# Routed experts' biases: from a one-hot matmul to broadcast rows added by VectorE, and a turning moved behind the next block's rows

## What is computed

```python
y = gelu(einsum('bsd,edf->bsef', x, g) + gb)      # rgb: [16, 256]
y = y * (einsum('bsd,edf->bsef', x, w1) + b1)     # rb1: [16, 256]
out = einsum('bsef,efd->bsed', y, w2) + b2        # rb2: [16, 512]
```

## Time and profile before

| | us |
|---|---|
| time before, median of 3 (1360.68 to 1362.64) | 1361.8 |
| the profiled execution | 1362.64 |
| its span in the trace | 1360.8 |
| TensorE busy in the span | 1321.8 (97%) |
| VectorE busy | 850.3 (62%) |
| ScalarE busy | 687.1 (50%) |

### The profile page before, as it was taken

One profiled execution on the slowest core, in us unless ns is written; L12 is line 12 of the kernel. 1 busy time (PEld: TensorE's weight loads), 2 busy tenths in 40 slices (PEclk: granted clock), 3 DMA queues, 4 the chain that ended last, 5 costly groups with the idle time before them and its releaser, 6 DMA issues. The chain is left out here.

```text
span 1360.8 us, 22755 instructions
## 1 busy us (share of the span) xinstructions
PE 1321.8 (97%) x6836; PEld 1102.7 (81%) x6836; DVE 850.3 (62%) x1753; ACT 687.1 (50%) x1615; POOL 384.3 (28%) x353
## 2 busy tenths in 40 slices
PE   6899999999999999999999999997999999999997
PEld 3667777888888888888888888886887888888886
DVE  5788755666666666666666777666666444344568
ACT  3334427666666666666666776663312323232232
POOL 0336465000013092030550302800032232323164
PEclk9999999999999999999999999999999999999999
DMA  9999989967677769696687899793646999894375
GB/s 290 382 343 375 369 299 319 341 223 237 205 276 272 237 231 327 206 341 207 226 301 268 289 316 329 278 354 146 246 156 244 336 347 363 289 368 172 128 235 171
DMA packets 160057, 375.57 MB, mean 276 GB/s; under 512 B 23164, under 2 KB 80576, under 8 KB 147696
## 3 DMA queue, kind: packets, MB, share of 16 engines
q1 hardware_dynamic: 144416, 314.32, 66.0%
q0 software_dynamic: 15568, 60.32, 12.5%
HBM read 245.84 MB, written 128.22 MB: 275 GB/s over the span
## 5 line engine op out<-in xcount | busy, mean ns | idle before, releaser
L1193 ACT ACTIVATE a_pr<-a_pr,a_stat 128x128 f32<-128x128 f32 (+3 forms) x256 | 141.9, 555 | 71.4 <-DVE a_stat L1272 71.4
L1212 ACT ACTIVATE a_pT<-x_banks 128x512 fp32r<-128x512 f32 (+1 forms) x192 | 87.1, 531 | 75.6 <-PE x_banks L1415 75.6
L1199 ACT ACTIVATE a_pr<-a_pr,a_stat 128x128 f32<-128x128 f32 (+3 forms) x256 | 122.3, 550 | 0.5 <-DVE a_stat L1277 0.5
L1399 PE MATMUL x_banks<-a_pT,a_cv 128*128 128x512 f32 (+1 forms) x576 | 120.5, 354 | 0.3 <-issue 0.3
L1399 PEld LDWEIGHTS x_banks<-a_pT,a_cv 128*128 128x128 f32 x576 | 103.4, 188 | 21.2 <-issue 0.7
L1272 DVE CUSTOM_DVE_ANT_0 a_pr<-a_psS,f_mask 128x256 f32<-128x256 f32 (+2 forms) x192 | 101.2, 555 | 23.7 <-PE a_psS L1387 23.3
L1300 DVE TENSOR_TENSOR a_pT<-x_banks,a_pT 128x512 fp32r<-128x512 f32 (+1 forms) x192 | 103.4, 594 | 12.6 <-ACT a_pT L1212 12.6
L101 PE MATMUL x_banks<-a_hT,a_wqk 128*128 (+1 forms) x256 | 99.9, 390 | 1.0 <-DVEq L1259 1.0
L102 PE MATMUL x_banks<-a_hT,a_wqk 128*128 (+1 forms) x256 | 99.7, 390 | 0.0
L103 PE MATMUL x_banks<-a_hT,a_wqk 128*128 (+1 forms) x256 | 99.6, 389 | 0.0
L1288 DVE SCALAR_TENSOR_TENSOR a_qT<-x_banks,a_qT 128x512 fp32r<-128x512 f32 x64 | 44.3, 692 | 85.6 <-ACT a_qT L1203 85.6
(11 more groups left out here) (378 smaller groups left out, 3611.9 us busy)
## 6 DMA issues: line engine op xcount, KB each, us to landing
w1s_d<-a_ws SPq DMA_DIRECT2D x72, 512.0 KB, 3.5
a_wqk<-wqk_d SPq DMA_DIRECT2D x64, 512.0 KB, 5.0
a_mh<-mhl_d SPq DMA_DIRECT2D x32, 1024.0 KB, 5.9
s_ring<-w1s_d SPq DMA_DIRECT2D x16, 2048.0 KB, 10.0
w2s_d<-a_ws SPq DMA_DIRECT2D x72, 256.0 KB, 3.9
qpe_d<-p_qs SPq DMA_DIRECT2D x16, 1024.0 KB, 5.1
a_rw<-in_L_ffn_rw SPq DMA_DIRECT2D x128, 128.0 KB, 3.5
a_qpe<-qpe_d SPq DMA_DIRECT2D x64, 256.0 KB, 2.7
```

The costliest lines, as they stand in the source:

```text
L1193: nc.scalar.activation(pr[i], pr[i], ACT.Exp, bias=nmax[:, i:i + 1], scale=-1.0, accum_out=rsum[:, i:i + 1]).then_inc(ex, 1)
L1199: nc.scalar.activation(pr[i], pr[i], ACT.Copy, scale=rinv[:, i:i + 1]).then_inc(nr, 1)
L1212: nc.scalar.activation(pT[:, u, 0, dst], src, ACT.Copy).then_inc(p_hi, 1)
L1399: last = nc.tensor.matmul(two_of(bank)[:, :, (2 - k) * P:2 * P], cv[:, j, cs], pT[:, :, ps, o:o + k * P], start=m == 0, stop=m == len(part ...
```

## The change

- **Biases.** `oh`, `bs`, the matmuls of lines 2419 and 2430, the making of `bs` ahead of the blocks and the one-hot row on ScalarE are gone. Instead SyncE loads, for each expert, 128 equal rows of its two first biases (tile `bg`, 128x512, 256 KB, from a new HBM tensor `b1_d` that holds both side by side) and of its second bias (`bo`, 128x512, 256 KB), into rings of three places as for the weights. The weights count as landed only with their biases.
- **VectorE** reads the place of the expert into a register (`row_of`, twice in a block), adds the bias to the gate part (into `y2`), adds it to the up part (into `y3`), multiplies `y3` with the gelu's result, and adds the second bias as it copies the result rows. The gelu reads and writes `y2` in SBUF.
- **Turning.** The two transposes of a block's activations (`turned`) move from the end of step k to step k+1, behind the four transposes of the rows of block k+2 and ahead of its first matmuls.
- The tiles `ys` and `lt` now lie in `bo`; the last updates of the shared experts use another temporary, with waits of their own; the second biases of the first three experts are loaded after the shared experts' last activations.

The diff, cut to its core:

```diff
+                def bias2(one, s, landed):
+                    sp.dma_start(bo[:, s], K.ins["L0_ffn_rb2"][one].broadcast_to([P, D])).then_inc(landed, 16)
+                def bias1(one, s, landed):
+                    sp.dma_start(bg[:, s], K.b1_d[one].broadcast_to([P, 2 * F])).then_inc(landed, 16)
...
                     sp.dma_start(ring1[:, s].rearrange("p c s n -> p (c s n)").bitcast(F32),
                                  K.w1s_d[bass.ds(e, 1)].rearrange("a p c s n -> (a p) (c s n)")).then_inc(rw1_in[s], 16)
+                    sp.wait_ge(gu_ok, done)
+                    bias1(bass.ds(e, 1), s, rw1_in[s])
...
+                    sp.wait_ge(yo_ok, done)
+                    bias2(bass.ds(e, 1), s, rw2_in[s])
...
-                    nc.scalar.activation(y2[:, u % 2], pg[:, u % 2, 0, 0:F], ACT.Gelu).then_inc(eg, 1)
+                    act.wait_ge(g_ok, k + 1)
+                    nc.scalar.activation(y2[:, u % 2], y2[:, u % 2], ACT.Gelu).then_inc(eg, 1)
...
+                def row_of(table, k):
+                    n = dve.value_load(slot[0:1, bass.ds(k, 1)], min_val=0, max_val=RS - 1)
+                    return table[:, bass.ds(n, 1)].rearrange("p a n -> p (a n)")
                 def rows(k, j, u):
+                    bias = row_of(bo, k)
                     dve.wait_ge(oo, k + 1)
...
-                    v.tensor_copy(yo[:, u % 2], po[:, u % 2]).then_inc(yo_ok, 1)
+                    tt_(yo[:, u % 2], po[:, u % 2], bias, ALU.add).then_inc(yo_ok, 1)
...
+                    bias = row_of(bg, k)
+                    dve.wait_ge(fo, k + 1)
+                    tt_(y2[:, u % 2], pg[:, u % 2, 0, 0:F], bias[:, 0:F], ALU.add).then_inc(g_ok, 1)
...
+                    tt_(y3[:, u % 2], pg[:, u % 2, 0, F:2 * F], bias[:, F:2 * F], ALU.add).then_inc(gu_ok, 1)
+                    dve.wait_ge(gu_ok, k + 1)
                     dve.wait_ge(eg, k + 1)
-                    tt_(y2[:, u % 2], pg[:, u % 2, 0, F:2 * F], y2[:, u % 2], ALU.mult).then_inc(em, 1)
+                    tt_(y2[:, u % 2], y3[:, u % 2], y2[:, u % 2], ALU.mult).then_inc(em, 1)
...
-                    pe.wait_ge(oh_ok, k + 1)
-                    nc.tensor.matmul(pg[:, u % 2, 0], oh[:, u], bs[:, 0], start=False, stop=True).then_inc(fo, 1)
...
-                    nc.tensor.matmul(po[:, u % 2], oh[:, u], bs[:, 1], start=False, stop=True).then_inc(oo, 1)
...
                     if k + 1 < NBLK:
                         trans(k + 1, (k + 1) // XS, (k + 1) % XS)
+                    if k:
+                        turned(k - 1, (k - 1) % XS)
                     ahead = gated(k, u, e, s)
```

More of the change, by code:

```diff
@@ L1556, in stage_ffn @@
         yo = N.t[:, 0:2]
-        y2 = N.t[:, 3].rearrange("p (u f) -> p u f", u=2)
+        y2, y3 = (N.t[:, n].rearrange("p (u f) -> p u f", u=2) for n in (3, 2))
         rev = small[:, 0:E]
@@ L1688, in _ @@
                 sp.wait_ge(taken, 1)
+                sp.wait_ge(b1_out, 32)
+                for e in range(RS):
+                    bias1(slice(e, e + 1), e, pre1_in[e])
                 weights(None, ring2[:, 0], 0, None, pre2_in[0])
-                sp.wait_ge(pre1_in[0], 16)
+                sp.wait_ge(y_lo, 2 * NU)
+                for e in range(RS):
+                    bias2(slice(e, e + 1), e, pre2_in[e])
+                sp.wait_ge(pre1_in[0], PRE1)
                 sp.sem_inc(landed1, 1)
-                sp.wait_ge(pre2_in[0], 16)
+                sp.wait_ge(pre2_in[0], 32)
                 sp.sem_inc(landed2, 1)
@@ L2412, in gated @@
                         nc.tensor.matmul(pg[:, u % 2, 0], xT[:, u % 2, 0, c], w(c, 1), start=False, stop=False)
-                        nc.tensor.matmul(pg[:, u % 2, 0], xT[:, u % 2, 1, c], w(c, 0), start=False, stop=False)
+                        last = nc.tensor.matmul(pg[:, u % 2, 0], xT[:, u % 2, 1, c], w(c, 0), start=False, stop=c == DC - 1)
                         if c == 1 and k + 1 < NBLK:
@@ L2417, in gated @@
                             ahead = (ahead, place(k + 1))
[L2418 to L2419 removed]
+                    last.then_inc(fo, 1)
                     return ahead
@@ L2428, in out, with turned @@
                         nc.tensor.matmul(po[:, u % 2], eT[:, u % 2, 0, f], w(f, 1), start=False, stop=False)
-                        nc.tensor.matmul(po[:, u % 2], eT[:, u % 2, 1, f], w(f, 0), start=False, stop=False)
-                    nc.tensor.matmul(po[:, u % 2], oh[:, u], bs[:, 1], start=False, stop=True).then_inc(oo, 1)
+                        last = nc.tensor.matmul(po[:, u % 2], eT[:, u % 2, 1, f], w(f, 0), start=False, stop=f == FC - 1)
+                    last.then_inc(oo, 1)
+                def turned(k, u):
+                    pe.wait_ge(em, k + 1)
+                    for f in range(FC):
+                        m = nc.tensor.transpose(py[:, f * PB:(f + 1) * PB], y2[:, u % 2, f * P:(f + 1) * P], K.ident[:, :])
+                    m.then_inc(et, 1)
                 def step(k, e, s, old):
@@ L2444, in step @@
                         part(1, 3, (3,)).then_inc(sh_o, 1)
-                    pe.wait_ge(em, k + 1)
-                    for f in range(FC):
-                        m = nc.tensor.transpose(py[:, f * PB:(f + 1) * PB], y2[:, u % 2, f * P:(f + 1) * P], K.ident[:, :])
-                    m.then_inc(et, 1)
                     return ahead
```

65 lines of the change are left out of this document (26 added, 39 removed).

## The result

The changed kernel takes **1350.97 us** (median of 1350.35 to 1353.39) against 1362.22 of the kernel before beside it: ratio 0.9928, 95% interval 0.9912 to 0.9943. The medians lie 11.3 us apart; by the ratio it is 9.8 us less, with 7.8 and 12.0 as the ends. A second series on another chip gave 1351.7 against 1360.39, ratio 0.9936 (0.9922 to 0.9951). The forecast was 1348, the range 1341 to 1358: right in direction and range, and 3 us too fast.

A forecast was written before the change was run, and what follows sets the result against it. TensorE was taken to bound the kernel, through its chain of turnings in the routed experts. Terms: -21.4 + 1 + 3.5 + 0.5 + 2 + 0.5 = -13.9, from 1361.8 to 1348 us; range 1341 to 1358.

The forecast's parts named there:

- Matmuls removed: TensorE, routed experts: 47 blocks lose two matmuls each, 94 x 0.228 = 21.4 us less; block goes to 4.77 us.
- The longer way to the product: VectorE's added bias additions before the product: no stall in most blocks, 1 us more allowed, bounds 0 to 9 us.
- product always late: Rival: each block's turning waits 0.2 us for VectorE's product, 9.2 us instead of 1, so 1356 us; chance 0.12.
- the text's own sign: Wrong on the product if the turning of the activations waits for VectorE in ordinary blocks.
- The slack of 0.12 to 0.27 us: Margin between the product's end and TensorE asking for it, at 2.06 us after the last first matmul's start (g).
- Why the turning's place matters: Turning behind the row transposes makes the product fit; at its old place, g + 1.60, it would stall.
- Blocks 40 to 43: VectorE has three more operations and no cover there: 0.6 to 1.6 us a block, 3.5 us more taken.
- The last two turnings: At the end, no next rows to turn: two turnings wait for the product 0.2 to 0.35 us each, 0.5 us.
- Transfers: Bias loads for 13 experts, 6.8 MB more: 2 us more, bounds 0 to 14; rival that they bind, about 1358, chance 0.13.
- Ahead of block 0: Bias loads before block 0's gather: between 0.5 us less and 3 us more, 0.5 us more taken.
- The sum: All terms over the whole kernel: 13.9 us less than 1361.8, giving 1348 us.
- VectorE's register loads: Two loads a block, say 0.6 us; rival: at 1.3 us for one load VectorE bounds, 1384 us, chance 0.06.

The follow-up runs named there:

- e1: Changed kernel with the activations' turning in blocks 1 to 46 placed after the block's first three first matmuls instead of ahead of them; 1344.85 us, ratio 0.9884.
- e3: Kernel before the change with only the turning of the activations moved behind the next block's row transposes; 1360.27 us, ratio 1.0003.
- e7: Changed kernel with TensorE's two register loads for the next block moved to the first group of the second matmuls; 1350.42 us, ratio 0.9919.
- e2: Changed kernel with the turning back at its old place, the end of the block's second matmuls (bias half alone); 1366.15 us, ratio 1.0041.
- e5: Changed kernel with the other stage's twelve operations of blocks 40 to 43 moved from VectorE to GpSimd, in blocks 8 to 19; 1349.23 us, ratio 0.9911.
- e6: Changed kernel with both the turning after the block's first three matmuls and the twelve operations on GpSimd; 1342.23 us, ratio 0.9864.
- e4: Changed kernel without the loads of both bias rows for experts 3 to 15 (26 transfers of 256 KB); 1352.85 us, ratio 0.9945.
- e8: Changed kernel with turning after three matmuls, twelve operations on GpSimd, and the last turning behind three matmuls of the next stage; 1341.3 us, ratio 0.9853.

## Why the prediction was right, and where it was not

**Matmuls removed** (forecast 21.4 us less): right. Where nothing else interferes (e1) the block takes 4.784 us, 0.446 less than before; times 47 that is 21.0.

**The longer way to the product** (forecast 1 us more): this is the step that failed. It measured 0.133 us a block (e1 against the changed kernel), 4.9 us over blocks 3 to 40 and some 6 over all. "No stall in most blocks" was wrong: the product is late in every ordinary block. The mechanism and its place stood in the text, and so did the rival "product always late" with 9.2 us; the rival is what came, at two thirds of its size. By the text's own sign (the turning waits for VectorE in ordinary blocks) the forecast was wrong on the product.

The slack of 0.12 to 0.27 us was mis-sized at both ends. The product was reckoned to end 1.73 to 1.88 us after g, the upper end with 0.15 us for an address computation; it ends 1.99 us after it. The addition starts at 0.54 instead of 0.43, because VectorE's queue computes an address between the wait and the addition (57 ns, the first row below, and some 0.05 to the addition's start): that lies within the allowance. The rest had none: the gelu from SBUF takes 0.42 instead of the 0.38 from PSUM, and the handovers to the gelu and to the product take 0.08 and 0.10 us, not 0.04 (ahead of the product the queue has one more wait, line 2130, 21 ns). And TensorE asks earlier than g + 2.06. That figure is nearly right for the turning's first matmul (g + 2.04 if nothing waits); but what waits for the product is its weight load, which starts with the fourth row transpose, 0.11 us earlier, as e3's rows show. In the changed kernel that transpose starts at g + 1.93, and the load at g + 2.04. So the load is 0.11 us late. Small errors, all of one sign, used up the slack.

VectorE's queue at the first addition and at its register loads (ns min/median/max):

```profile
L2125 DVEq FUSED_REGOPS  x47: 57/57/71, 1041.2 to 1271.2; - x47
```

```profile
L2104 DVEq FUSED_REGOPS  x139: 53/190/206, 1039.7 to 1274.1; - x139
L2104 DVEq TENSOR_LOAD <-s_slot x94: 298/305/556, 1039.1 to 1273.8; - x94
```

The price of the late product was not worked out in the text. Against e3 less its two bias matmuls (5.230 - 0.459 = 4.771 us) the changed kernel's block of 4.917 is 0.146 us longer: the three distances at the turning grew by 0.07 us (121, 154 and 39 ns against 109, 109 and 28), the matmul behind them by 0.02 (334 against 315), the queue's lost lead costs 0.035 (e7), and some 0.02 are spread over the other matmuls. The lateness is thus not paid twice at the turning; it is the lost lead that comes on top. e1, at 4.784, comes within 0.013 of the block without a wait.

**Why the turning's place matters**: the sentence that at its old place it would stall was right (e2: 0.50 us a block, slower than before).

**Blocks 40 to 43** (3.5 us): right in size. 32.32 us less six blocks of 4.784 is 3.6; taking the operations away gave 2.7 beside a late product (e5) and 3.9 without one (e1 to e6), and another 1.0 and 0.7 in the stretch behind turning 46 (next paragraph). Three of the blocks carry it (5.81, 6.06 and 5.71 us), the forecast had four at 5.7.

**The last two turnings** (0.5 us): they wait 0.45 us each, 0.9 us, by the same late product. The turnings behind turning 46 of the rows and the last second matmul:

```profile
1263.03 0.44 PE L2448 MATMUL s_pl<-ident,n_t 128*128 128x128 f32 x2 [0.82 <-DVE n_t L2131]
...
1267.96 0.44 PE L2448 MATMUL s_pl<-ident,n_t 128*128 128x128 f32 x2 [0.28 <-DVE n_t L2131]
...
1272.86 0.44 PE L2448 MATMUL s_pl<-ident,n_t 128*128 128x128 f32 x2 [0.31 <-DVE n_t L2131]
...
1277.04 0.39 PE L2442 MATMUL s_po<-s_ring,s_eT 128*128 x1
```

From turning 46 to that matmul it is 15.43 us in both profiles of the changed kernel, against 13.89 before. Four matmuls less and two transposes more, which the turning's new place brings into this stretch, would make it 0.7 shorter, so it is 2.2 us too long. The last two turnings make 0.9 of that. The first row is the turning of block 44, about 1.0 us late: it still waits behind the other stage's operations of blocks 40 to 43, and with these on GpSimd (e5) the stretch takes 14.44. The remaining 0.3 is about the ordinary price of two more blocks. Behind the last second matmul the two profiles take 71.5 and 70.5 us against 71.1: scatter.

**Transfers** (2 us, bounds 0 to 14): 0 within what can be measured (e4). 417 GB/s were said to be wanted, and the changed kernel moved 416 over 90 us at a share of 1.02 without a single wait of TensorE for weights. The rule cited from the Trainium skill ("DMA: Bandwidth & Descriptors", "Where 436 GB/s comes from"), 358 GB/s at the HBM side, is not what this core met. Another page of the Trainium skill, "HBM Reference", "Specifications (TRN2)", says that a core that streams alone measures about 425 GB/s, and the rows agree with that. What the transfers do cost is a late store now and then: in e4, e6, e7 and e8 the blocks in which the result rows waited 2.0 to 2.5 us were 0.3 to 1.8 us longer. The changed kernel's five waits (1.6 us at most, against one of 1.1 before) made no block longer, and e4 shows that they come without the biases' loads too.

**Ahead of block 0** (0.5 us): the wait for the gather was 0.78 us and is 0.53 here:

```profile
1035.39 0.41 PE L2409 MATMUL s_px<-ident,n_rows 128*128 128x128 f32 x2 [0.53 <-DMA n_rows<-h_d,s_tri]
```

In the second profile it is 0.89 us, and 1.24 in e3 with the old code, so no effect of the change can be told; the scatter ahead of it is larger still. Blocks 0 to 2, which the forecast took for ordinary, gained 0.3 us. Three matmuls and two transposes fewer stand between their turnings, 0.9 us; but the turning of block 0 waits for its product there:

```profile
1042.78 0.20 PEld L2448 LDWEIGHTS s_pl<-ident,n_t 128*128 128x128 f32 x2 [0.72 <-DVE n_t L2131]
```

In e1, e6 and e8, where it comes later, this stretch takes 11.3 to 11.4 us, 0.8 to 0.9 less than before.

**The sum.** That 1348 came within some 4 us is in part an offset: the product cost 5 us more than its term, the transfers 2 us less than theirs. The chain and the first term were right, the total was helped by luck.

**VectorE's register loads** (rival, 1384 us): 0.31 us for the load and 0.19 for its address by the medians above, within the 0.6 us assumed, and mostly beside the instruction before. In ordinary blocks VectorE has cover; in 40 to 43 it has none, as foreseen.

## What to carry to other kernels

When work moves from the engine that bounds to one that feeds it, reckon the feeding path to 0.05 us per step, with every handover and address computation, and put the consumer's request later by more than the error: here one matmul's worth (0.23 us) in front of the request was worth 6 us. A producer that is late by a tenth of a microsecond shows up in no list of waits; the distances between starts, slot by slot against a kernel with the same order that doesn't wait (e3, not e1), show it. Ask which instruction waits: here it was the weight load, 0.11 us ahead of its matmul. And two halves of a change can be worth less than nothing apart: try each alone.

## What the runs showed of the hardware

An addition on VectorE that waits for a matmul and takes an operand by a register starts 0.54 us after that matmul's start. One with fixed addresses, in the attention of the same program, starts after 0.43 (26 of 26 such waits at line 1311), as ScalarE's gelu did:

```profile
270.26 0.40 PE L104 MATMUL x_banks<-a_mh,a_oT 128*128 128x512 f32 x1
...
270.69 0.69 DVE L1311 TENSOR_TENSOR n_acc<-x_banks,n_acc 128x512 f32<-128x512 f32 x1 [0.68 <-PE x_banks L104]
```

GpSimd takes 1.31 us for a 128x512 sum or product of SBUF operands, twice VectorE's 0.69, and ran twelve of them beside VectorE's work at a price of at most 0.4 us (e5) and 1 us (e6) in the other blocks:

```profile
L1797 POOL TENSOR_TENSOR n_h<-n_h,s_gb 128x512 f32<-128x512 f32 x4 | 5.2, 1311 | 0.1
```

(This row is of e5, 1070 to 1160 us: count, busy us, mean ns, idle before.) And a switch between the matmuls of the weights and transposes costs next to nothing: the first matmul after transposes takes 0.31 us to the next start instead of 0.23, but the last transpose ahead of it takes 0.03 instead of 0.11. Where transposes interrupt the block twice (e1) the block is within 0.013 us of e3's, which has one interruption, less the bias matmuls.
